# Attention on one core: the values' matmuls put ahead of the weighted values, and the key copies ahead of the second exponentials

## What is computed

```python
def _attention(x, W_q, W_k, W_v, W_o):        # 16 heads of 16 channels, 64 tokens
    b, l, dm = x.shape
    d_head = dm // N_HEADS
    scale = sqrt(N_HEADS / dm)
    def split(y):
        return y.reshape(b, l, N_HEADS, d_head).transpose(0, 2, 1, 3)
    q, k, v = split(x @ W_q.T), split(x @ W_k.T), split(x @ W_v.T)
    attn = jax.nn.softmax(scale * jnp.einsum('bnqd,bnkd->bnqk', q, k), axis=-1)
    o = jnp.einsum('bnqk,bnkd->bnqd', attn, v)
    return o.transpose(0, 2, 1, 3).reshape(b, l, dm) @ W_o.T
...
x = x + a_alpha * _attention(_ada_rmsnorm(x, t, attn_gamma_w, attn_beta_w), W_q, W_k, W_v, W_o)
```

## Time and profile before

| what | before |
|---|---|
| time, median of 3 runs | 752.47 us (752.31 to 752.88) |
| the profiled execution: its own time | 751.87 us |
| the profiled execution: span | 750.1 us |
| TensorE matmul busy | 730.3 us, 97% |
| VectorE busy | 519.7 us, 69% |
| GpSimd busy | 418.4 us, 56% |
| ScalarE busy | 364.3 us, 49% |
| mean granted TensorE clock | 0.996 of full speed |

### The profile page before, as it was taken

One profiled execution on the slowest core, in us unless ns is written; L12 is line 12 of the kernel. 1 busy time (PEld: TensorE's weight loads), 2 busy tenths in 40 slices (PEclk: granted clock), 3 DMA queues, 4 the chain that ended last, 5 costly groups with the idle time before them and its releaser, 6 DMA issues.

```text
span 750.1 us, 18076 instructions
## 1 busy us (share of the span) xinstructions
PE 730.3 (97%) x6406; PEld 596.6 (80%) x6406; DVE 519.7 (69%) x803; ACT 364.3 (49%) x721; POOL 418.4 (56%) x408
## 2 busy tenths in 40 slices
PE   8999999999999899999999999999999999999994
PEld 6888888888888799999988777677777767778883
DVE  3977778777789889888895465646655666453455
ACT  4344444444447687888874333233323332322584
POOL 4666646656678888999987533324242423320353
PEclk9999999999999999999999999999999999999998
DMA  8955344454434000000004355577757668769943
GB/s 240 297 107 106 86 114 110 105 119 115 100 80 73 15 34 3 3 0 0 2 3 132 101 181 177 157 225 213 212 167 256 202 206 255 229 179 388 363 172 113
DMA packets 80666, 105.69 MB, mean 141 GB/s; under 512 B 39744, under 2 KB 52896, under 8 KB 80480
## 3 DMA queue, kind: packets, MB, share of 16 engines
q1 hardware_dynamic: 79456, 103.32, 47.2%
q10 hardware_dynamic: 1152, 1.59, 1.0%
HBM read 75.23 MB, written 21.26 MB: 129 GB/s over the span
## 4 chain that ended last, share of the span: by engine, by line
PE 88%; POOL 4%; DVE 3%; issue 2%; DMA 1%; ACT 1%; SPq 0%; POOLq 0%; DVEq 0%; ACTq 0%
PE banks L435 23%; PE banks L1202 22%; PE banks L1232 12%; PE banks L1048 5%; PE banks L1254 4%; PE banks L452 4%; PE banks L1125 3%; PE banks L1083 3%; PE banks L1166 2%; PE banks L1107 2%; PE banks L1141 2%; PE banks L1827 2%; PE banks L1854 2%; DMA early<-in_up_t 1%; PE banks L472 1%
## 5 line engine op out<-in xcount | busy, mean ns | idle before, releaser
L1584 DVE TENSOR_TENSOR g<-banks,silu 128x512 f32<-128x512 f32 x64 | 44.1, 689 | 78.9 <-PE banks L1202 51.1
L1588 DVE TENSOR_TENSOR g_lo<-g,g_hi 128x512 fp32r<-128x512 f32 x64 | 57.9, 904 | 47.5 <-ACT g_hi L1424 47.5
L1424 ACT ACTIVATE g_hi<-g 128x512 fp32r<-128x512 f32 x64 | 40.4, 631 | 98.3 <-DVE g L1584 97.3
L1418 ACT ACTIVATE silu<-banks 128x512 f32<-128x512 f32 x64 | 38.2, 597 | 97.7 <-PE banks L1202 97.7
L435 PE MATMUL banks<-up_hi,xs_hi 128*128 128x512 f32 x256 | 82.1, 402 | 2.5 <-ACT up_hi L598 1.7
L435 PE MATMUL banks<-up_lo,xs_hi 128*128 128x512 f32 x256 | 79.5, 391 | 0.1
L435 PE MATMUL banks<-up_hi,xs_lo 128*128 128x512 f32 x256 | 79.2, 391 | 0.0
L1202 PE MATMUL banks<-mlp_in_hi,w_hi 128*128 128x512 f32 x252 | 78.8, 393 | 0.0
L1202 PE MATMUL banks<-mlp_in_lo,w_hi 128*128 128x512 f32 x252 | 78.0, 391 | 0.0
L1202 PE MATMUL banks<-mlp_in_hi,w_lo 128*128 128x512 f32 x252 | 77.8, 390 | 0.0
L659 DVE SCALAR_TENSOR_TENSOR h<-banks,rstd,gelu 128x512 f32<-128x512 f32 x64 | 47.9, 748 | 34.4 <-ACT gelu L552 33.8
(11 more groups left out here) (223 smaller groups left out, 1803.9 us busy)
## 6 DMA issues: line engine op xcount, KB each, us to landing
gen_hyper<-in_gen_t SPq DMA_DIRECT2D x32, 512.0 KB, 4.4
gen_made<-base_w SPq DMA_DIRECT2D x64, 256.0 KB, 4.7
adapter_w<-gen_made SPq DMA_DIRECT2D x64, 256.0 KB, 4.3
tokens<-in_x_tok SPq DMA_DIRECT2D x32, 128.0 KB, 2.5
w_stage<-in_w_t SPq DMA_DIRECT2D x32, 128.0 KB, 2.5
tokens_again<-in_x_tok SPq DMA_DIRECT2D x32, 128.0 KB, 2.3
weight_slot<-adapter_w SPq DMA_DIRECT2D x4, 1024.0 KB, 8.9
x_sb<-in_x_t SPq DMA_DIRECT2D x7, 512.0 KB, 6.8
```

The source lines that it names most:

```text
L1418: nc.scalar.activation(silu[:, f % 2, :], chunk_bank(s, f, 0)[:, :], ACT.Silu).then_inc(S["silu_done"], 1)
L1424: nc.scalar.activation(gs[0][:, f % 2, :], g[:, f % 2, :], ACT.Copy).then_inc(S["g_hi_done"], 1)
L1584: nc.vector.tensor_tensor(g[:, f % 2, :], chunk_bank(s, f, 1)[:, :], silu[:, f % 2, :], ALU.mult).then_inc(S["g_done"], 1)
L1588: nc.vector.tensor_tensor(gs[1][:, f % 2, :], g[:, f % 2, :], gs[0][:, f % 2, :].bitcast(FP32), ALU.subtract).then_inc(S["g_ready"], 1)
```

## The change

In the steps t = 8 to 16 (`beside_scores`):

- `weighted_ps`: the weighted values go into bank 1, from which ScalarE copies the keys, and no longer into bank 6.
- TensorE: `values` runs ahead of `weighted_values`, which then stands directly ahead of the next step's `scores`. `weighted_values` waits for `k_done` in addition, since it overwrites the keys' bank.
- `transposes(s, 0)` of the step behind such a one (t = 9 to 17) no longer waits for `ot_done`. `output`, which comes next, still does.
- ScalarE: `take_keys` runs ahead of the second exponentials and no longer behind them. `take_queries` stays behind them.

The other steps keep their order, banks and waits. Nothing is added to the work or taken from it.

```diff
@@ -859,8 +859,12 @@
+        def beside_scores(s):
+
+            return not isinstance(s.t, int) or PEELED <= s.t <= NA
+
         def weighted_ps(s):
-            return bank[7 if s.last(3) else 6].rearrange("p (c t) -> p c t", c=2)
+            return bank[7 if s.last(3) else 1 if beside_scores(s) else 6].rearrange("p (c t) -> p c t", c=2)
...
@@ -1116,7 +1120,7 @@
-                if two == 0:
+                if two == 0 and not beside_scores(Step(s.t - 1, s.k, NA)):
                     wait(pe, A["ot_done"], s.at(3) if s.live(4) else 0)
...
@@ -1132,6 +1136,8 @@
                 pe.wait_ge(A["v_high_done"], s.at(3) + 1)
+                if beside_scores(s):
+                    pe.wait_ge(A["k_done"], s.at(1) + 1)
...
@@ -1176,11 +1182,14 @@
                 queries(s)
+                if beside_scores(s):
+                    values(s)
                 weighted_values(s)
...
-                values(s)
+                if not beside_scores(s):
+                    values(s)
...
@@ -1400,10 +1409,13 @@
+                if beside_scores(s):
+                    take_keys(s)
                 if not first_two:
                     exponentials(s, 1)
+                if not s.first_tile(3) and not beside_scores(s):
+                    take_keys(s)
                 if not s.first_tile(3):
-                    take_keys(s)
                     take_queries(s)
```

## The result

| | before | after |
|---|---|---|
| time, median of 13 runs each | 752.37 us | 754.29 us |
| ratio, with its 95% interval | | 1.0032 (1.0024 to 1.0041) |
| the profiled execution: its own time, span | 751.87, 750.1 us | 754.48, 752.6 us |
| T1 of t = 8 to T1 of t = 17 | 90.77 us | 93.49 us |

The account below looks back on a forecast made before the run. TensorE was taken to set the pace, with GpSimd right behind. +0.8 (first turn), +0.6 (seven steady turns) and +0.3 (last turn) sum to +1.7 us: 754.2 us against the median of 752.47, range 752.2 to 755.8.

Parts of the forecast that it names:

- The first turn: Turn from t = 8 to 9: last rstd pair on ScalarE delays value copies and next scores; +0.8 us.
- W to O: Weighted values to output projection in a steady turn: 3.31 us, including a 0.30 stall for the value copies.
- release: Time from the end of the awaited value copy to the output projection's start on TensorE: 0.05 us.
- T1 to W: Second transposes to weighted values: grows by 1.42 us, from 3.83 to 5.25, as the values move in between.
- The last turn: Turn of t = 17, where VectorE makes two of the four value copies behind ot_lo: +0.3 us.
- W to S: Weighted values to next scores: nearest row 1.03 us, deviation between -0.24 and +0.24, taken as 0.
- The wait for ot_done that T0 loses: First transposes no longer wait for VectorE's low half of the weighted values: worth 0, at most 0.2 us a step.
- the early key copies: ScalarE's key copies ahead of the second exponentials delay these by some 0.7 us, at no cost to the turn.
- the third rival: Second exponentials become the bound, softmax slips: 0.2 to 0.3 us more in each of eight steps, 756.2 us; chance 0.10.
- The first: Rival: only TensorE's boundaries count, output projection not held, step 0.21 us shorter, -1.9 us, 750.6 us; chance 0.12.
- The second rival: Steady steps as forecast or a little cheaper, t = 8 costs little, scores of t = 9 on time: 753.2 us; chance 0.18.
- The fourth: Rival: stall and boundary gain cancel, both special turns too, so no gain or cost: 752.5 us; chance 0.08.

Follow-up runs that it names:

- short copies: Changed kernel, but each of ScalarE's value copies in plain steps takes 32 of 256 columns, part of the computation left out; ratio 1.0018 (1.0007 to 1.0029).
- the better wait order: Changed kernel with the output projection's wait for y_alpha put ahead of those for ot_done and the value copies, which come last; ratio 1.0031 (1.0016 to 1.0045).
- the early-keys run: Changed kernel with the key copies put back behind the second exponentials, as before the change; ratio 1.0093 (1.0074 to 1.0111).

## Why the prediction was right, and which terms were off

**The mechanism is shown.** O was held by the value copies, these by ot_hi, and this by W. The profile has the wait at O in the steady turns without a loop return, with the loop written out in seven of seven; short copies take it away and put O at W + 3.02, where TensorE alone was said to need 3.01. The first turn is held by the logarithm at S and the copies at O (4.35 after W, and 4.25 with short copies, by S alone; the sum had 4.21 and 4.2), and starting a step later removes its cost. That putting the logarithm ahead of ot_hi and VectorE's copies ahead of ot_lo brings both special turns back is shown in one run with the better wait order, not each by itself.

**The mis-sized terms.**
- *W to O, 3.31 in the sum, 3.46 measured.* Its pieces: W to ot_hi 1.16 (1.17 said), ot_hi to the end of the fourth copy 2.05 (2.09 said), release 0.22 to the weight load and 0.03 more to the matmul (0.05 said). The 0.05 came from the earlier trace rows, where the late wait is the only one. Where it is the last of several it took 0.12 (the copies' in the better order, the keys' in the early-keys run), and with a fulfilled one behind it 0.22: the whole of the missing release is on record, why an engine takes it isn't. Against 3.31 that is +0.15 in each of seven turns; T1 to W came out at 5.22 for 5.25. Together +0.19 a turn for +0.08, more than twice the forecast.
- *The first turn, +1.00 for +0.8.* W to O 4.35 for 4.21, the same release; T1 to W +1.48 for +1.42.
- *The last turn, +0.42 for +0.3.* W to O 3.65 for 3.45, again the release behind VectorE's copy: 387.50 - (386.81 + 0.43) = 0.26.

**The forecast's closeness is partly luck.** The steps add up to +1.7 and the profile's stretch shows +2.72. The ratio stands for +2.4 (1.8 to 3.1), the difference of the two medians for +1.92, and the forecast's base was 752.47, 0.10 over the later median. The mechanism and the sign were right. The size, +1.7, is near the medians' +1.92 and just under the ratio's interval; by the profile's measure the sum was 1.0 short, so the last 0.1 isn't earned.

**What was costed at nothing.** W to S was taken at 1.03, and is 1.03 where no loop return lies between. The return itself (0.45) wasn't foreseen; the hold covered it, as the prediction said that it would cover a later S. The wait for ot_done that T0 loses was worth at most 0.15 in the whole stretch, "0, at most 0.2 a step": right. No run has the early key copies alone, but in the changed kernel T1 never waits for p_sb (1.49 to 1.53 after O), so they cost nothing there and the second exponentials didn't become the bound; the third rival is out.

**The rivals.** The first was wrong in what it took for granted, that "GpSimd would allow it": with the copies out of the way T1 waits for the second normalisation, and with that moved too, the loop's return costs 0.9 in two of the turns. Its 9.78 a turn exists, and makes the seven turns 0.72 shorter, but its 750.6 doesn't follow from it: the first turn of 11.75 and the last of 10.73 leave the stretch 1.0 longer than in the kernel before. The second rival fell with the S of t = 9, 1.2 late. The fourth didn't come true: all three kinds of turn are longer.

## What to carry to other kernels

When work is moved along the order of one engine, work out anew when the engine that copies its results can start, in that engine's own order: here the value copies ended 0.36 ahead of O (355.07, 355.43) and now end 3.21 after W, 0.2 behind the point where TensorE would be ready for O, since they stand behind a copy that waits for W. Before a gain on the busiest engine is counted, follow each second ring (here GpSimd's, 0.07 short of binding) through that gain; here one wait after another took the place of the one removed. And a waiting instruction's release should be read from one with the same set of waits in the same order.

## What the runs showed of the hardware beyond that

- TensorE's hardware loop costs 0.45 at its return where 64 small matmuls stand on either side of it (W to S 1.48 for 1.03, the rest put down to issue), 0.11 to 0.14 where the loop is left, and nothing of it with the loop written out. In the kernel before, with V behind W, no such gap was in the turn of 9.99.
- TensorE's weight load starts 0.05 after the end of the awaited copy where that wait is its only one, 0.11 to 0.12 where it is the last of several, and 0.22 to 0.23 where a fulfilled one stands behind it. It was the same with VectorE's copy in t = 17: 0.22, and 0.11 in the better order.
- On GpSimd an elementwise operation starts 0.19 to 0.20 late when it works on the output of the one just before. With another's work between, the pause is filled: that was 10.04 against 9.85 a turn.
